# V and K traffic on the GpSimd DMA queue, and one attention step per FFN step, in a fused attention and FFN kernel

## The chip, the cores and the metric

The kernel runs on all 8 cores of one Trainium2 chip. Every core runs the same program on its own quarter of one batch element's rows, and the cores don't exchange anything. The metric is the time of the slowest core in microseconds (us); lower is better.

## The reference

One sandwich layer over x of shape (2, 8192, 1024) in float32: an attention with sigmoid weights, then a five-matrix FFN, each with a layer norm before and after and a residual.

```python
q, k, v = (proj(Wq), proj(Wk), proj(Wv))            # 16 heads of 64
scores = einsum('bhqd,bhkd->bhqk', q, k) * SCALE
w = sigmoid(scores)
w = w / (w.sum(axis=-1, keepdims=True) + EPS)
out = einsum('bhqk,bhkd->bhqd', w, v) ... @ Wo.T
h = silu(x @ w1.T * s1) * (x @ w2.T * s2)            # 1024 -> 4096
h = gelu(h @ h1.T * hs1)                             # 4096 -> 4096
h = gelu(h @ h2.T * hs2)                             # 4096 -> 4096
return h @ w3.T * s3                                 # 4096 -> 1024
# layer: x = x + ln(attention(ln(x)));  x = x + ln(ffn(ln(x)))
```

## The kernel before

Five instruction streams (PE, ACT, DVE, SP, GpSimd) are written out by hand. `emit(eng, fn, waits, incs)` appends one piece to a stream: the engine waits for the semaphore values in `waits`, then runs `fn`. Each stream is executed strictly in the order in which it was emitted. `"sy"` is SP's stream and DMA queue, `"gp"` is GpSimd's (POOL in the profile). A barrier makes SP wait for everything, then all engines for SP.

A core holds S = 8192 rows of x (transposed) and computes the T = 2048 query rows that are its own. The order of the work:

- **Projection stage** (`phase0`), four super-tiles of 2048 rows. Each: the layer norm's statistics (eight loads of `xs`, Square on ACT, sums on PE), the normalised `lnb` (eight more loads of `xs`), K projection (eight blocks, DVE copies to `kvo`, DMA to `K_sc` in HBM, L367), in the first also Q, then V projection: 16 blocks of 128 rows, 16 matmuls each, a DVE cast to `vvo` (L416; two buffers), and a DMA to `V_sc` (L431). This DMA writes rows of 65 bf16 (130 B): 128 partitions x 16 heads = 2048 pieces.
- **Attention A** (`gen_phase1` with `kct` = 3), 2 blocks of 512 queries x 8 head pairs. For each head pair one load of `kbuf` (2 MB, L520), then tiles of key chunks. A tile is: for each of the two heads, score matmuls into `psS` (L561), one sigmoid on ACT into `wtil` (L573), and then the value matmuls of the *previous* tile into `psO` (L600). Every 8 key chunks two loads of `vbuf` (130 KB each, L546; four slots, two per head). At the end of the head pair two row sums go out (`RS_sc`, L625).
- **phase2** for 1024 rows: output projection, layer norm, residual, `y1`. Its last part goes over eight row blocks: load of `xb` (L758), three DVE operations (L762, L765, L768), store of `y1t` to `y1_sc` (L774), statistics.
- **Mixed stage**: attention B (`kct` = 2, one `kbuf`, the other 2 blocks of 512 queries) and FFN A are two generators whose pieces are taken in turn (L219 to L232): two `yield`s of attention, one of the FFN. Attention B has 16 head pairs x 33 = 528 yields (32 tiles of 2 key chunks and a closing one). FFN A has two halves of 512 rows with 232 yields each: w1 32 (8 matmuls, Silu on ACT), w2 32 (8 matmuls, DVE), h1 and h2 64 each (16 matmuls, and a Gelu every second yield), w3 24 (two with 16 matmuls, one without), 8 for statistics, 8 for the output. That makes 464. Its weights come by casting DMAs on GpSimd's queue into two buffers `wfb` (L837): 256 KB each for w1 and w2, 1 MB for h1, h2 and w3; each waits for the matmuls of the weight block two before it.
- **phase2** for the other 1024 rows, then **FFN B** over them in one go.

The semaphores `st_v0` and `st_v1` are used by the V stores of the projection stage and again by the `RS_sc` stores.

Of the kernel before, what the change touches and what calls it, by code (L numbers as in the profile page):

```python
# [20 lines left out]
class Builder:  # L21
# [70 lines left out]
    def build(self):  # L92
# [26 lines left out]
        for s in ["bar", "pe", "act", "dve", "gp",  # L119
                  "ld_x0", "ld_x1",  # L120
                  "ld_w0", "ld_w1", "ld_w2",
                  "ld_k0", "ld_k1",
                  "ld_v0", "ld_v1", "ld_v2", "ld_v3",
                  "ld_y0", "ld_y1",
                  "ld_c",
                  "st_k0", "st_k1",
                  "st_v0", "st_v1",
                  "st_y0", "st_y1",
                  "st_rs",
                  "st_o0", "st_o1"]:  # L130
            self.sem(s)

# [81 lines left out]
        if qms_b:  # L214
            with ExitStack() as pctx:
                psS, psO = p1_psums(pctx, 2, nkb=1)
                g_mid = self.gen_phase1(qms_b, 2, psS, psO)
                g_ffn = gen_ffn_a()
                mid_alive = ffn_alive = True  # L219
                while mid_alive or ffn_alive:  # L220
                    if mid_alive:
                        for _ in range(2):
                            try:
                                next(g_mid)
                            except StopIteration:
                                mid_alive = False
                                break
                    if ffn_alive:
                        try:
                            next(g_ffn)  # L230
                        except StopIteration:
                            ffn_alive = False  # L232
        else:
            for _ in gen_ffn_a():
                pass
# [18 lines left out]
    def phase0(self):  # L254
# [4 lines left out]
        with ExitStack() as sc:  # L259
# [10 lines left out]
            for b in range(2):  # L270
                for hh in range(NH):
                    self.emit("gp", lambda e, b=b, hh=hh: e.memset(
                        vvo[b][:, hh * (DH + 1) + DH: hh * (DH + 1) + DH + 1], 1.0),
                        incs=[("gp", 1)])
# [12 lines left out]
            for sup in range(NSUP):  # L287
                ts0 = sup * TSUP
# [54 lines left out]
                with ExitStack() as pctx:  # L343
                    psP = [pctx.enter_context(nc.psum_tensor(self.u(f"psP{i}"), [128, TSUP], F32))
                           for i in range(2)]
                    psP_free = [[], []]
                    for oc in range(NCD):
                        par = oc % 2

                        def mk_kproj(e, o=oc, p=par, psP=psP):  # L350
                            for ic in range(NCD):
                                for tt in range(NTT):
                                    inst = e.matmul(  # L353
                                        psP[p][:, tt * NT:(tt + 1) * NT],
                                        wkb[:, ic * D + o * 128: ic * D + o * 128 + 128],
                                        lnb[:, ic * TSUP + tt * NT: ic * TSUP + (tt + 1) * NT],
                                        start=(ic == 0), stop=(ic == NCD - 1))
                            return inst
                        self.emit("pe", mk_kproj,
                                  waits=[("dve", ln_ready), ("ld_w0", wproj_ready)] + psP_free[par],  # L360
                                  incs=[("pe", 1)])
                        mmv = self.c("pe")
                        self.emit("dve", lambda e, p=par, psP=psP: e.tensor_copy(kvo[p][:], psP[p][:]),
                                  waits=[("pe", mmv)] + kvo_free[par], incs=[("dve", 1)])
                        psP_free[par] = [("dve", self.c("dve"))]
                        dvv = self.c("dve")
                        self.emit("sy", lambda e, p=par, o=oc, ts0=ts0: e.dma_start(  # L367
                            self.K_sc[o, :, ts0:ts0 + TSUP], kvo[p][:]),
                            waits=[("dve", dvv)], incs=[(f"st_k{par}", 16)])
                        kvo_free[par] = [(f"st_k{par}", self.c(f"st_k{par}"))]  # L370
                    if sup == 0:
                        NTTQ = T // NT
                        for oc in range(NCD):
                            par = oc % 2

                            def mk_qproj(e, o=oc, p=par, psP=psP):
                                for ic in range(NCD):
                                    for tt in range(NTTQ):
                                        inst = e.matmul(
                                            psP[p][:, tt * NT:(tt + 1) * NT],  # L380
                                            wqb[:, ic * D + o * 128: ic * D + o * 128 + 128],
                                            lnb[:, ic * TSUP + tt * NT: ic * TSUP + (tt + 1) * NT],
                                            start=(ic == 0), stop=(ic == NCD - 1))
                                return inst
                            self.emit("pe", mk_qproj,
                                      waits=[("dve", ln_ready), ("ld_w0", wproj_ready)] + psP_free[par],
                                      incs=[("pe", 1)])
                            mmv = self.c("pe")
                            self.emit("dve", lambda e, p=par, o=oc, psP=psP: e.tensor_copy(
                                self.qbuf[:, o * T:(o + 1) * T], psP[p][:, 0:T]),  # L390
                                waits=[("pe", mmv)], incs=[("dve", 1)])
                            psP_free[par] = [("dve", self.c("dve"))]

                with ExitStack() as pctx:
# [3 lines left out]
                    for tk in range(TSUP // 128):  # L398
# [26 lines left out]
                        def mk_vst(e, p=par, tkg=tkg, NKC_ALL=NKC_ALL):  # L425
# [3 lines left out]
                            src = bass.AP(vvo[p], 0,  # L429
                                          [[NH * (DH + 1), 128], [DH + 1, NH], [1, DH + 1]])  # L430
                            return e.dma_start(dst, src)  # L431
                        self.emit("sy", mk_vst, waits=[("dve", dvv)], incs=[(f"st_v{par}", 16)])
                        vvo_free[par] = [(f"st_v{par}", self.c(f"st_v{par}"))]

    def alloc_rows(self, scope, W, tag):
# [57 lines left out]
    def gen_phase1(self, qms, kct, psS, psO):  # L493
# [14 lines left out]
        if True:  # L508
# [7 lines left out]
            for qm in qms:  # L516
                q0 = qm * QM
                for hp in range(NCD):
# [20 lines left out]
                    for ti, (kc0, nk) in enumerate(tiles):  # L539
                        for kc in range(kc0, kc0 + nk):  # L540
                            if kc % 8 == 0:
                                kb = kc // 8
                                for hh in range(2):
                                    vslot = hh * 2 + kb % 2
                                    self.emit("sy", lambda e, hh_=2 * hp + hh, kb=kb, p=vslot:
                                              e.dma_start(vbuf[p][:], bass.AP(  # L546
                                                  self.V_sc.tensor,
                                                  hh_ * 128 * NKC_ALL * (DH + 1) + kb * 8 * (DH + 1),
                                                  [[NKC_ALL * (DH + 1), 128],
                                                   [1, 8 * (DH + 1)]])),  # L550
                                              waits=vbuf_free[vslot],
                                              incs=[(f"ld_v{vslot}", 16)])
                                    v_lds[(hh, kb)] = self.c(f"ld_v{vslot}")
# [65 lines left out]
                    for hh in range(2):  # L619
                        h = 2 * hp + hh  # L620
                        self.emit("dve", lambda e, hh=hh: e.tensor_copy(  # L621
                            rs_row[hh][:], psO[hh][64:65, :]),
                            waits=[("pe", pv_all)] + rs_free[hh], incs=[("dve", 1)])
                        rsd = self.c("dve")
                        self.emit("sy", lambda e, hh=hh, h=h, q=q0: e.dma_start(  # L625
                            self.RS_sc[h:h + 1, q:q + QM], rs_row[hh][:]),
                            waits=[("dve", rsd)], incs=[(f"st_v{hh}", 16)])
                        rs_free[hh] = [(f"st_v{hh}", self.c(f"st_v{hh}"))]
                        self.emit("dve", lambda e, hh=hh, c=hp, q=q0: e.tensor_copy(
                            self.obuf[hh * 64:hh * 64 + 64, c * T + q: c * T + q + QM],  # L630
                            psO[hh][0:64, :]),
                            waits=[("pe", pv_all)], incs=[("dve", 1)])
                        psO_free[hh] = [("dve", self.c("dve"))]
# [3 lines left out]
    def phase2(self, t0, TW, ln2t):  # L637
# [4 lines left out]
        with ExitStack() as sc:  # L642
# [27 lines left out]
            with ExitStack() as pctx:  # L670
# [3 lines left out]
                for c in range(NCD):  # L674
                    par = c % 2
# [73 lines left out]
            with ExitStack() as pctx:  # L749
# [6 lines left out]
                for ic in range(NCD):  # L756
# [14 lines left out]
                        incs=[("dve", 1)])  # L771
                    dvv = self.c("dve")
                    xb_free[par] = [("dve", dvv)]
                    self.emit("sy", lambda e, i=ic, p=par, t0=t0, y1t=y1t: e.dma_start(  # L774
                        self.y1_sc[i, :, t0:t0 + TW], y1t[p][:]),
                        waits=[("dve", dvv)], incs=[(f"st_y{par}", 16)])
                    self.emit("act", lambda e, p=par, sq2=sq2, y1t=y1t: e.activation(
# [367 lines left out]
```

How the kernel before makes its waits and increments, by code:

```python
        def closure(e, fn=fn, wl=wl, il=il):  # L49
            for h, v in wl:
                e.wait_ge(h, v)
            inst = fn(e) if fn is not None else None
            for h, n in il:
                assert inst is not None
                inst.then_inc(h, n)
```

## Time and profile before

| | us |
|---|---|
| median of 2 runs | 8227.16 (8216.3 and 8238.03) |
| the profiled execution | 8052.45 |
| its slowest core (6), from first to last instruction | 8050.9 |
| spans of the eight cores | 7983.0 to 8050.9 |
| projection stage | 0 to 1745 |
| attention A | 1745 to 3050 |
| phase2 | 3050 to 3230 |
| mixed stage | 3230 to 6448 |
| phase2 | 6450 to 6620 |
| FFN B | 6620 to 8050 |

All rows are of core 6. The stage bounds are read from the first and last instructions of each stage's lines. In the profile PE is the matmul row of TensorE and PEld its weight loads; a matmul's own duration is modelled and overlaps its neighbours, so rates are read from the distance between starts. "DMA share" is the mean busy share of the 16 DMA engines.

### The profile page before, as it was taken

To read this page: it belongs to the slowest core of one execution; us is meant where nothing else is said; L and a number is where in the kernel's file an instruction comes from. 1 tells how busy PE (TensorE), PEld (TensorE's weight loads), DVE (VectorE), ACT (ScalarE), POOL (GpSimd) and SP (SyncE) were. 2 spreads that over 40 slices of the span, in tenths; PEclk is the share of its full clock that TensorE was granted. 3 is DMA by queue.
4 is the path that set the end of the run, shared out by engine and by line. 5 is a ranking of instruction groups with operands and counts; after the bars stand their busy time and mean duration, and the time that the engine had idled before them with its cause. 6 is when DMAs were issued, how large, how long until landed. Compare 5 with 4: busy or idle time off the path is not lost.

```text
span 8050.9 us, 66197 instructions; the slowest of 8 cores (7983.0 to 8050.9 us)
## 1 busy us (share of the span) xinstructions
PE 5763.5 (72%) x22567; PEld 2173.6 (27%) x22904; DVE 806.9 (10%) x659; ACT 2656.6 (33%) x2394; POOL 221.1 (3%) x453
## 2 busy tenths in 40 slices
PE   5645354547878786568788788766688757899996
PEld 1212121212222222112222222212233213344442
DVE  2112031300000003001000000010100140100002
ACT  1000000026777772565555555466100011000000
POOL 0000000000000000000000000000100001000000
PEclk7867676778989897779999999987999969999898
DMA  4778777681111112223434333322566524444343
GB/s 125 24 67 58 62 62 64 61 32 57 48 58 48 58 48 61 59 58 71 91 81 83 87 82 83 74 59 48 80 125 127 111 76 62 72 75 77 68 74 76
DMA packets 298831, 570.25 MB, mean 71 GB/s; under 512 B 151328, under 2 KB 216864, under 8 KB 257952
## 3 DMA queue, kind: packets, MB, share of 16 engines
q1 hardware_dynamic: 239056, 278.65, 22.6%
q0 software_dynamic: 59472, 287.34, 20.7%
q8 instruction: 217, 3.56, 0.2%
q14 instruction: 86, 0.70, 0.0%
HBM read 802.49 MB, written 50.72 MB: 106 GB/s over the span
## 4 chain that ended last, share of the span: by engine, by line
PE 53%; DMA 24%; ACT 11%; issue 8%; DVE 4%; SPq 0%; ACTq 0%; DVEq 0%; POOLq 0%
PE psG L902 20%; DMA V_sc<-vvo 10%; PE psS L561 9%; ACT wtil L573 8%; PE psO L600 8%; PE psF L857 5%; DMA kbuf<-K_sc 3%; DMA wfb<-h 3%; PE psP L353 3%; DMA wfb<-w 3%; DMA xs<-xT 3%; PE psW L939 3%; PE ps_sum L306 1%; ACT L573 1%; DMA xb<-xT 1%
## 5 line engine op out<-in xcount | busy, mean ns | idle before, releaser
L573 ACT ACTIVATE wtil<-psS 128x1024 bf16<-128x1024 f32 (+1 forms) x1728 | 1935.7, 1180 | 945.9 <-PE psS L561 941.2
L902 PE MATMUL psG<-fb,wfb 128*128 128x512 bf16 x8005 | 1845.2, 389 | 100.8 <-DMA wfb<-h 80.8
L561 PE MATMUL psS<-qbuf,kbuf 64*128 64x512 bf16 x4096 | 1033.1, 404 | 827.8 <-ACT wtil L573 487.6
L600 PE MATMUL psO<-wtil,vbuf 128*65 128x512 bf16 x4096 | 1140.6, 411 | 12.0 <-ACT wtil L573 12.0
L902 PEld LDWEIGHTS psG<-fb,wfb 128*128 128x128 bf16 x8192 | 814.3, 100 | 1129.3 <-issue 280.7
L561 PEld LDWEIGHTS psS<-qbuf,kbuf 64*128 64x128 bf16 x4096 | 244.2, 95 | 1546.7 <-issue 1470.4
L404 PE MATMUL psV<-wvb,lnb 128*128 128x512 bf16 x1004 | 325.6, 495 | 444.7 <-DVE vvo L416 432.0
L600 PEld LDWEIGHTS psO<-wtil,vbuf 128*65 128x65 bf16 x4096 | 407.2, 116 | 689.0 <-issue 462.7
L300 ACT ACTIVATE sq<-xs 128x2048 bf16<-128x2048 f32 x32 | 61.2, 1911 | 1238.1 <-DMA xs<-xT 1238.1
L621 DVE COPY rs_row<-psO 1x512 f32<-1x512 f32 x64 | 43.8, 684 | 3093.6 <-PE psO L600 3092.5
L353 PE MATMUL psP<-lnb,wkb 128*128 128x512 bf16 x1000 | 227.2, 388 | 158.5 <-DVE lnb L337 157.4
L857 PE MATMUL psF<-ln2tA,wfb 128*128 128x512 bf16 x976 | 292.7, 446 | 61.1 <-DMA wfb<-w 49.4
L915 ACT ACTIVATE fb<-psG,hs2b 128x512 bf16<-128x512 f32 (+1 forms) x96 | 79.7, 830 | 677.8 <-PE psG L902 677.4
L404 PEld LDWEIGHTS psV<-wvb,lnb 128*128 128x128 bf16 x1024 | 120.1, 121 | 650.2 <-issue 598.8
L306 PE MATMUL ps_sum<-xs,onesF 128*1 128x512 f32 x256 | 145.0, 720 | 200.3 <-ACT sq L300 200.3
L857 PE MATMUL psF<-ln2tB,wfb 128*128 128x512 bf16 x1003 | 233.1, 386 | 76.6 <-DMA wfb<-w 66.2
L915 ACT ACTIVATE fb<-psG,hs1b 128x512 bf16<-128x512 f32 (+1 forms) x96 | 79.7, 830 | 629.5 <-PE psG L902 629.1
L939 PE MATMUL psW<-fb,wfb 128*128 128x512 bf16 x1001 | 226.0, 383 | 15.3 <-DMA wfb<-w 9.3
L573 ACT ACT_TABLE_LOAD x128 | 164.2, 1283 | 210.6 <-PE psS L561 209.5
L952 DVE TENSOR_SCALAR fbf<-psW,s3b 128x512 bf16<-128x512 f32 (+1 forms) x24 | 22.3, 929 | 1877.3 <-PE psW L939 1621.8
L857 PEld LDWEIGHTS psF<-ln2tA,wfb 128*128 128x128 bf16 x1024 | 116.1, 116 | 243.2 <-issue 177.0
L353 PEld LDWEIGHTS psP<-lnb,wkb 128*128 128x128 bf16 x1024 | 101.9, 100 | 288.1 <-issue 172.8
(103 smaller groups left out, 2116.0 us busy)
## 6 DMA issues: line engine op xcount, KB each, us to landing
wfb<-h POOLq DMA_DIRECT2D x192, 1024.0 KB, 8.2
vbuf<-V_sc SPq DMA_DIRECT2D x512, 130.0 KB, 2.7
xs<-xT SPq DMA_DIRECT2D x64, 1024.0 KB, 4.8
kbuf<-K_sc SPq DMA_DIRECT2D x32, 2048.0 KB, 8.2
wfb<-w POOLq DMA_DIRECT2D x192, 256.0 KB, 3.8
wfb<-w POOLq DMA_DIRECT2D x24, 1024.0 KB, 8.3
V_sc<-vvo SPq DMA_DIRECT2D x64, 260.0 KB
K_sc<-kvo SPq DMA_DIRECT2D x32, 512.0 KB, 2.6
```

The source lines that it names most:

```text
L300: lambda e, p=par: e.activation(sq[p][:], xs[p][:], AF.Square),
L306: e.matmul(ps_sum[0:1, tt * NT:(tt + 1) * NT], self.onesF[:], xs[p][:, tt * NT:(tt + 1) * NT], start=(i == 0), stop=(i == NCD - 1))
L353: inst = e.matmul(psP[p][:, tt * NT:(tt + 1) * NT], wkb[:, ic * D + o * 128: ic * D + o * 128 + 128], lnb[:, ic * TSUP + tt * NT: ic * TSU ...
L404: inst = e.matmul(psV[p][:, oh * NT:(oh + 1) * NT], lnb[:, ic * TSUP + t * 128: ic * TSUP + t * 128 + 128], wvb[:, ic * D + oh * NT: ic * ...
L561: inst = e.matmul(psS[hh][:, j * QM:(j + 1) * QM], kbuf[kp][b:b + 64, (k0 + j) * 128:(k0 + j + 1) * 128], self.qbuf[b:b + 64, hp_ * T + q0 ...
L573: self.emit("act", lambda e, w=w, hh=hh, n=nk: e.activation(wtil[w][:, 0:n * QM], psS[hh][:, 0:n * QM], AF.Sigmoid, scale=ATT_SCALE), wait ...
L600: inst = e.matmul(psO[hh][:, :], vbuf[vslot][:, a_ * (DH + 1): a_ * (DH + 1) + DH + 1], wtil[w][:, j * QM:(j + 1) * QM], start=(k == 0), s ...
L621: self.emit("dve", lambda e, hh=hh: e.tensor_copy(rs_row[hh][:], psO[hh][64:65, :]), waits=[("pe", pv_all)] + rs_free[hh], incs=[("dve", 1)])
L857: inst = e.matmul(psF[p][:, tt * NT:(tt + 1) * NT], wfb[b][:, ic * 128:(ic + 1) * 128], ln2t[:, ic * ln2_w + off + tt * NT: ic * ln2_w + o ...
L902: inst = e.matmul(psF[p][:, tt * NT:(tt + 1) * NT], wfb[b][:, ic * 128:(ic + 1) * 128], s[:, ic * th + tt * NT: ic * th + (tt + 1) * NT], ...
L915: self.emit("act", lambda e, o=oc, p=par, d=dstb, sc_=scl, psF=psF: e.activation(d[:, o * th:(o + 1) * th], psF[p][:], AF.Gelu, scale=sc_[ ...
L939: inst = e.matmul(psF[p][:, tt * NT:(tt + 1) * NT], wfb[b][:, ic * 128:(ic + 1) * 128], fb1[:, ic * th + tt * NT: ic * th + (tt + 1) * NT] ...
```

## The change

Five edits. The K and V stores of the projection stage (L367, L431), the 512 loads of `vbuf` (L546) and the 16 stores of `y1t` (L774) are issued by GpSimd instead of SP. The stores of the row sums get semaphores of their own, `st_r0` and `st_r1`. In the mixed stage one attention yield is taken per FFN yield, not two.

```diff
-                  "st_rs",
+                  "st_rs", "st_r0", "st_r1",
...
                     if mid_alive:
-                        for _ in range(2):
-                            try:
-                                next(g_mid)
-                            except StopIteration:
-                                mid_alive = False
-                                break
+                        try:
+                            next(g_mid)
+                        except StopIteration:
+                            mid_alive = False
...
-                        self.emit("sy", lambda e, p=par, o=oc, ts0=ts0: e.dma_start(
+                        self.emit("gp", lambda e, p=par, o=oc, ts0=ts0: e.dma_start(
                             self.K_sc[o, :, ts0:ts0 + TSUP], kvo[p][:]),
...
-                        self.emit("sy", mk_vst, waits=[("dve", dvv)], incs=[(f"st_v{par}", 16)])
+                        self.emit("gp", mk_vst, waits=[("dve", dvv)], incs=[(f"st_v{par}", 16)])
...
-                                    self.emit("sy", lambda e, hh_=2 * hp + hh, kb=kb, p=vslot:
+                                    self.emit("gp", lambda e, hh_=2 * hp + hh, kb=kb, p=vslot:
                                               e.dma_start(vbuf[p][:], bass.AP(
...
-                            waits=[("dve", rsd)], incs=[(f"st_v{hh}", 16)])
-                        rs_free[hh] = [(f"st_v{hh}", self.c(f"st_v{hh}"))]
+                            waits=[("dve", rsd)], incs=[(f"st_r{hh}", 16)])
+                        rs_free[hh] = [(f"st_r{hh}", self.c(f"st_r{hh}"))]
...
-                    self.emit("sy", lambda e, i=ic, p=par, t0=t0, y1t=y1t: e.dma_start(
+                    self.emit("gp", lambda e, i=ic, p=par, t0=t0, y1t=y1t: e.dma_start(
                         self.y1_sc[i, :, t0:t0 + TW], y1t[p][:]),
```

## Rows read from the trace of the kernel before

**Rows 1.** Windows by stage: length, busy of each engine, PE clock, DMA share, GB/s.
```profile
core 6: us, PE busy (x) PEld busy (x) DVE busy (x) ACT busy (x) POOL busy (x), PEclk, DMA share, GB/s
282.00:500.00 218.00, 85.54 (x251) 30.95 (x256) 20.02 (x17) 0.00 (x0) 0.00 (x0) 0.67 1.13 19
...
3261.00:5681.00 2420.00, 1805.31 (x7063) 626.70 (x7178) 92.84 (x133) 1409.54 (x1413) 89.50 (x169) 0.88 0.33 71
5683.00:6448.00 765.00, 581.93 (x2522) 247.71 (x2574) 49.26 (x69) 52.63 (x77) 54.07 (x102) 0.95 0.64 115
...
3823.00:5019.00 1196.00, 944.97 (x3924) 344.89 (x3989) 22.63 (x33) 677.77 (x679) 33.47 (x64) 0.92 0.40 84
...
7387.00:7506.00 119.00, 118.42 (x542) 53.93 (x552) 0.00 (x0) 8.91 (x8) 4.24 (x8) 1.00 0.40 72
```

**Rows 2.** Timeline of DVE in the first V projection: third and last cast of 16.
```profile
305.98 1.23 DVE L416 CAST vvo<-psV 128x1024 bf16<-128x1024 f32 x1 [13.18 <-DMA V_sc<-vvo]
...
493.37 1.23 DVE L416 CAST vvo<-psV 128x1024 bf16<-128x1024 f32 x1 [11.91 <-DMA V_sc<-vvo]
```

**Rows 3.** Timeline of POOL, mixed stage: one weight load each of w1, w2, h1, w3.
```profile
3354.28 0.53 POOL L837 DMA_DIRECT2D wfb<-w  x1 [9.87 <-PE psS L561]
3691.43 0.53 POOL L837 DMA_DIRECT2D wfb<-w  x1 [5.54 <-PE psS L561]
3923.28 0.53 POOL L837 DMA_DIRECT2D wfb<-h  x1 [16.34 <-PE psO L600]
5152.67 0.53 POOL L837 DMA_DIRECT2D wfb<-w  x1 [19.40 <-PE psS L561]
```

**Rows 4.** Timeline of PE (first row) and ACT, mixed stage, h1, around one Gelu.
```profile
3929.33 0.59 PE L561 MATMUL psS<-qbuf,kbuf 64*128 64x512 bf16 x2 [1.61 <-ACT wtil L573]
...
3924.25 0.69 ACT L915 ACTIVATE fb<-psG,hs1b 128x512 bf16<-128x512 f32 x1
3926.86 1.28 ACT L573 ACT_TABLE_LOAD   x1 [1.93 <-PE psS L561]
3928.16 3.85 ACT L573 ACTIVATE wtil<-psS 128x1024 bf16<-128x1024 f32 x4
```

**Rows 5.** Timeline of PE where a head pair ends.
```profile
5211.33 1.24 PE L561 MATMUL psS<-qbuf,kbuf 64*128 64x512 bf16 x4 [10.69 <-DMA kbuf<-K_sc]
```

**Rows 6.** Timeline of POOL after attention B ended: first and last of 62 h1/h2 loads.
```profile
5805.58 0.53 POOL L837 DMA_DIRECT2D wfb<-h  x1 [15.27 <-PE psG L902]
...
6311.27 0.53 POOL L837 DMA_DIRECT2D wfb<-h  x1 [7.13 <-PE psG L902]
```

**Rows 7.** Timeline of ACT, w3: two tiles back to back without FFN work between.
```profile
5132.89 1.94 ACT L573 ACTIVATE wtil<-psS 128x1024 bf16<-128x1024 f32 x2 [0.20 <-PE psS L561]
5135.09 1.94 ACT L573 ACTIVATE wtil<-psS 128x1024 bf16<-128x1024 f32 x2 [0.27 <-PE psS L561]
```

**Rows 8.** Page: DMA issues, with KB each and median us from issue to landing.
```profile
wfb<-h POOLq DMA_DIRECT2D x192, 1024.0 KB, 8.2
vbuf<-V_sc SPq DMA_DIRECT2D x512, 130.0 KB, 2.7
...
wfb<-w POOLq DMA_DIRECT2D x192, 256.0 KB, 3.8
```

**Rows 9.** Page: packets by size, software queue; tile wfb: POOL's DMA instruction, min/median/max ns.
```profile
DMA packets 298831, 570.25 MB, mean 71 GB/s; under 512 B 151328, under 2 KB 216864, under 8 KB 257952
...
q0 software_dynamic: 59472, 287.34, 20.7%
...
L837 POOL DMA_DIRECT2D wfb<-h x192: 530/530/539, 3817.5 to 7825.3; - x192
```

**Rows 10.** Timeline of PE where the second super-tile's statistics begin.
```profile
512.23 5.48 PE L306 MATMUL ps_sum<-xs,onesF 128*1 128x512 f32 x8 [39.64 <-ACT sq L300]
```

**Rows 11.** Waits, whole span: who waited, for whom, us in total, times, longest us.
```profile
DVE y1t L768 <- DMA xb<-xT: 43.1, 14, 4.7
```

## The prediction

> **What bounds the kernel now.** I read the times of the cores first (all within 0.9%, so one core may stand for all), then the windows by stage, then the timeline inside each stage that the change touches. The reader is to see three things.
>
> First, in the V projection PE is busy 85.5 of 218 us while the DMA engines are full at 19 GB/s [rows 1]. The third to the sixteenth cast into `vvo` come (493.37 - 305.98) / 13 = 14.4 us apart and each waits for a V store [rows 2]. So a V store costs 14.4 us of the DMA engines, in four super-tiles.
>
> Second, the mixed stage has two parts: 2420 us in which two attention tiles go with each FFN step, and 765 us in which the FFN is alone because attention B has run out [rows 1]. A matmul at full clock is 119 / 542 = 0.2196 us [rows 1]. A tile has 8 matmuls (1.75 us), an h step 16 (3.5 us), a w1 or w2 step 8 (1.75 us). The distance between weight loads gives the cadence; add 0.53 to the idle time in brackets: w1 10.40 us, w2 6.07, h 16.87 per block of two steps, w3 19.93 per block [rows 3]. PE work alone would be 5.25, 5.25, 14.0 and 17.5. The rest is the ping-pong: with two tiles in a row the second tile's scores wait for the first one's sigmoid, 1.61 us where a table load lies before it [rows 4]. Around each Silu and Gelu ACT loads a table twice, 1.28 us each. Where a head pair ends, PE stands 10.7 us for the single `kbuf` [rows 5].
>
> Third, in the part where the FFN is alone, h blocks come (6311.27 - 5805.58) / 61 = 8.3 us apart [rows 6], against 7.0 us of matmuls: weights bound it, and ACT idles.
>
> **The change, part by part.** The largest is the ratio of 1:1. FFN A has 464 steps, attention B 528. After the change 464 pairs of one tile and one FFN step run, then 64 attention steps alone. Only one tile stands between FFN steps, so its sigmoids are hidden behind the FFN's matmuls. Step by step:
>
> - w1, 64 steps. ACT needs per step a table load, a Silu, a table load and two sigmoids: 1.29 + 0.70 + 1.29 + 1.95 = 5.2 us, from the durations of [rows 4] with the Gelu's for the Silu. PE needs 3.5. ACT bounds; I take 5.3. 64 x 5.3 = 339, and two to three head pair ends of about 8 each (ACT catches up part of the 10.7): 362.
> - w2, 64 steps: PE 3.5, ACT 1.95, DVE less. 64 x 3.5 = 224, two ends at 10.7: 245.
> - h, 128 blocks of two steps: PE 2 x (1.75 + 3.5) = 10.5; ACT 4 x 0.97 + 1.29 + 0.70 + 1.29 = 7.2. After a Gelu the next sigmoid is done 0.1 + 1.29 + 0.70 + 1.29 + 0.97 = 4.35 us after the matmuls, and its `psS` is wanted after 5.25, so PE doesn't wait. 128 x 10.5 = 1344. Before, the window of h had 1196 us for 63 cadences of 16.87 = 1063 us: 12.5% on top for `kbuf` and low-clock stretches (clock 0.92) [rows 1]. The same share gives 168: 1512.
> - w3, 16 blocks of three tiles and 32 matmuls: 12.25 + 0.5 for the one pair of tiles left in a row; with two ends 227.
> - Statistics, 16 steps of tile and Square at 3.7: 64. Two row computations at 15: 30. Output, 16 steps at the pace of sigmoids, 2.2 us a tile [rows 7]: 40.
> - New: at the output of half 0 the DVE chain (about 4 us per row block, 32 us) is no longer covered by 16 tiles but by 8, and the first w1 load of half 1 waits for it: 17.
> - The 64 steps alone: 62 tiles x 2.2 = 136 and two ends: 156. Drain: 8.
>
> The sum is 362 + 245 + 1512 + 227 + 64 + 30 + 40 + 17 + 156 + 8 = 2661 us, against 3187 from the same start (2420 + 2 + 765). Gain: 526. That ACT gets some 128 more table loads (half 1's Gelus now stand between sigmoids), 164 us, is in the sum: in h ACT has 3 us to spare per block.
>
> The `vbuf` loads go behind weight loads on one queue. GpSimd then waits in order. A V load waits for value matmuls four steps back; a weight load waits for the block two before, which ended two steps back (w) or three (h). So the V load is issued at least two steps before its turn and wanted one step after it: over 10 us in w, over 15 in h. It lands in 2.7 us, behind a 1 MB load in about 8.2 + 0.8 more [rows 8]. A weight load in h has 3 tiles + one block of matmuls = 12.2 us before it is wanted, and lands in 8.2; in w 5.25 against 3.8 [rows 8]. Cost 0; if the cover in w1 and w2 were gone, 128 steps would each pay up to 1 us. In attention A no V load is waited for by PE now, and three tiles of slack remain: 0. SP's `kbuf` loads stay behind the `RS_sc` stores as they were, so the 10.7 us at each head pair stay too. The new semaphores cost nothing: they only part two uses that lie in different stages.
>
> The V stores are the unknown. Their 64 x 2048 = 131072 pieces make up most of the 151328 packets under 512 B [rows 9]. The queue that GpSimd issues to has 413 DMAs and 59472 packets now, 144 each, and POOL spends 530 ns on one [rows 9]; no row shows it with 2048 pieces. If all of the 530 ns went with the 128 rows, 2048 pieces would take 16 x 0.53 = 8.5 us of POOL; if none did, 0.53. Both are below 14.4, and with two buffers one store can be prepared while the other drains, so I take 0. The ends: preparing and draining one after the other, 8.5 us on each of the 56 waiting casts, +476; or stores that drain as fast as they can be prepared, (14.4 - 8.5) x 56 = 330 less. K stores (32 of 128 rows) take POOL 0.53 us each, and a block of 32 matmuls (7 us) lies over each: 0.
>
> DVE is busy for 20 of the 218 us of a V projection [rows 1]. The Trainium skill (SBUF — State Buffer, section SBUF: two separate sides) speaks against the move: DMAs issued from GpSimd starve while DVE runs an operation that takes the port pair the two share, and the page advises SP's or ACT's queue. By that rule the worst is those 20 us in each of four super-tiles, 80 in all; whether this cast from PSUM takes that port no row here shows. The sum goes without it.
>
> With the V stores off SP, the first two `xs` loads of a super-tile no longer stand behind the last store. PE's sums now begin at 512.23 [rows 10]; they must wait for the last cast, done at 493.37 + 1.23 = 494.6 [rows 2]. That is 17.6 us, less some competition with the stores still draining: 13 x 3 super-tiles = 40.
>
> In phase2 an `xb` load stood behind the `y1t` store of the block before, and DVE waited 43.1 us for it in all [rows 11]. With the store on GpSimd that wait goes, and about 8 come back since the store's landing now gates `y1t`: 35.
>
> Sum: 526 + 40 + 35 = 601. 8052 - 601 = 7451 us in the profiled execution's own terms. The median of the runs is 8227.16 / 8052.45 = 1.0217 of it, so the number to compare is 7451 x 1.0217 = 7613, say 7610.
>
> **Rivals.** *GpSimd bounds the V projection* (the one that can end slower). Place: the 56 casts that wait for a store. For it: 2048 pieces in a pattern of three dimensions is not what the 530 ns row shows. Against: even at the full 8.5 us the DMA engines' 14.4 last longer. Serial with the drain, at 22.9 us a store, it costs 476: 7927, times 1.0217 8099, 1.6% under now. The point from which the kernel is slower by 2% is 8391 / 1.0217 = 8213, so (8213 - 7451) / 56 = 13.6 us more, 28 us a store, or 1.75 us of POOL per 128 pieces, 3.3 times the row. At 35 us a store it would be 7451 + 1150 = 8601, times 1.0217 8790.
>
> *Queueing spoils the 1:1 stage*: weight loads come late behind V loads and `kbuf`. For it: w has only 1.4 us of slack. Against: DMA share 0.40 in h [rows 1]. If w paid 1 us and h blocks 1.5 us each: 128 + 192 = 320 less gain, 7771 x 1.0217 = 7940.
>
> *The clock eats it*: PE is busier, and the clock in the mixed stage was 0.88, alone 0.95 [rows 1]. Against: w2 and h cadences are constant at full clock apart from head pair ends. At 0.88 over the whole 2100 us of matmuls: up to 150 less, 7601, times 1.0217 7766. *V stores run faster on the other queue*, at 8.5 us: 330 more, 7121, times 1.0217 7276. Nothing in the rows speaks for it but the ends of the bound.
>
> **How the numbers follow.** As summed, with small misses either way 0.66; GpSimd as the bound 0.14 (0.07 up to 24 us a store, 0.07 beyond); queueing 0.08; clock 0.08; faster stores 0.04. Two per cent is about what a measurement of this kernel can tell. Faster by over 2%: the first and the last three, 0.86, and a little of the GpSimd case (under 22 us), 0.02; within 2%: 0.05; slower: 0.07. Range: 7330 (the runs at the profile's 7451 and some of the faster stores) to 7830 (the clock's loss, a third of the way to the serial stores). Below it lie most of the faster stores, above it half of the queueing case and most of the GpSimd case.
>
> **What would show it.** Windows: mixed stage 2660 us long with no FFN-only part of 765. POOL's weight loads 5.3 (w1), 3.5 (w2) and 10.5 us (h) apart. V casts still 14.4 us apart and POOL at most 8.5 us at a V store. First sums of a super-tile within 5 us of the last cast. `y1t` not waiting for `xb`. Wrong, if POOL is solid with V stores, if PE waits for `wfb` or `vbuf` in the mixed stage, or if h blocks take over 12 us.

## The result, and the profile after

The changed kernel takes 7522.61 us (median of 12 runs, 7297.37 to 7749.68), the kernel before 8241.57 us (median of 10 beside them): ratio 0.8957, 95% interval 0.8856 to 0.9058. That is faster by 10.4%; forecast were 7610 us and 7.5%.

In some executions, the changed kernel's profiled one among them (its cores 4 to 7), cores of one die or both run at a lower clock; the two medians count these executions, while ratios, and the times of the experiments below, leave them out. Readings from here on, of either kernel, are of core 2 where nothing else is said. The quotient of the two medians is 0.913, that of core 2's spans 0.911, and runs repeated below give 0.907 to 0.909, just above the interval; so the change is worth nearer 9% than 10.4%, and why the first ratio came out lower stayed open. Cores of the changed kernel, spans and granted clock:

```profile
core 2: 7278.4 us, clock 0.872
...
core 7: 7418.9 us, clock 0.854
die 0 (median of its cores): 7278.4 us, clock 0.872
die 1 (median of its cores): 7376.8 us, clock 0.854
```

On core 2 the kernel before spans 7992.0 us, the changed one 7278.4: 714 us less. The windows tell where they were. The stages in order are projection, attention A, phase2, mixed stage, phase2, FFN B; columns as in [rows 1]. Before:

```profile
0.00:1717.00 1717.00, 844.49 (x2776) 304.23 (x2776) 360.92 (x188) 77.75 (x42) 3.77 (x43) 0.73 0.76 63
1717.00:3017.00 1300.00, 1021.85 (x4112) 354.70 (x4112) 43.80 (x64) 945.16 (x706) 0.00 (x0) 0.90 0.17 53
3017.00:3232.00 215.00, 125.43 (x308) 40.81 (x308) 86.69 (x68) 27.75 (x27) 0.54 (x1) 0.67 0.27 81
3232.00:6424.00 3192.00, 2404.16 (x9756) 877.65 (x9756) 142.41 (x202) 1463.04 (x1491) 144.18 (x272) 0.90 0.41 81
6424.00:6622.00 198.00, 118.57 (x280) 38.06 (x280) 86.83 (x68) 20.72 (x20) 0.53 (x1) 0.67 0.25 75
6622.00:7992.00 1370.00, 1247.31 (x5672) 553.58 (x5672) 86.05 (x69) 121.28 (x109) 72.09 (x136) 0.97 0.40 74
```

After:

```profile
0.00:1680.00 1680.00, 833.48 (x2776) 300.78 (x2776) 361.22 (x188) 77.69 (x41) 95.09 (x139) 0.73 0.49 64
1680.00:2975.00 1295.00, 1020.55 (x4114) 354.75 (x4115) 43.79 (x64) 945.30 (x706) 138.14 (x257) 0.90 0.16 53
2975.00:3180.00 205.00, 118.78 (x300) 39.77 (x298) 87.19 (x68) 25.82 (x25) 5.91 (x12) 0.68 0.29 84
3180.00:5733.00 2553.00, 2199.80 (x9765) 835.79 (x9766) 142.51 (x202) 1627.51 (x1620) 283.83 (x527) 0.92 0.50 102
5733.00:5919.00 186.00, 111.28 (x280) 37.41 (x278) 87.45 (x68) 21.97 (x21) 4.69 (x9) 0.70 0.29 80
5919.00:7278.00 1359.00, 1244.00 (x5672) 552.28 (x5672) 86.04 (x69) 121.05 (x109) 72.23 (x136) 0.97 0.41 75
```

The reader is to see: of the 714 us, 639 are the mixed stage's, 37 the projection stage's, 22 the two phase2's. The remaining 16 lie in attention A and FFN B, where next to nothing was changed. PE has the same matmuls but 204 us less busy time in the mixed stage (91 of them in the scores, 47 in the value matmuls), ACT 164 us more (the table loads of half 1), POOL 140 us more.

Inside the mixed stage, POOL's weight loads of the changed kernel, w1, w2 and h1 (the rows answering to [rows 3]; the distance from one start to the next is the load's 0.53 plus the idle time, and 1.10 more where V loads stand between):

```profile
3244.11 0.54 POOL L835 DMA_DIRECT2D wfb<-w  x1 [4.71 <-PE psF L855]
3249.36 0.53 POOL L835 DMA_DIRECT2D wfb<-w  x1 [4.71 <-PE psF L855]
...
3405.89 0.54 POOL L835 DMA_DIRECT2D wfb<-w  x1 [2.70 <-PE psS L559]
3409.18 0.53 POOL L835 DMA_DIRECT2D wfb<-w  x1 [2.75 <-PE psS L559]
...
3577.76 0.54 POOL L835 DMA_DIRECT2D wfb<-h  x1 [9.42 <-PE psO L598]
3578.29 1.10 POOL L544 DMA_DIRECT2D vbuf<-V_sc  x2
3587.75 0.54 POOL L835 DMA_DIRECT2D wfb<-h  x1 [8.36 <-PE psO L598]
```

So w1 steps come 5.25 us apart, w2 steps 3.29 in these rows and mostly 3.25, h blocks 9.99 in these rows (median 9.95). Against forecasts of 5.3, 3.5 and 10.5 the first holds and the others are too long. From the first and last loads of each part:

| | before | forecast | after |
|---|---|---|---|
| w1, 64 steps | 660 | 362 | 330 |
| w2, 64 steps | 340 | 245 | 244 |
| h1 and h2, 128 blocks | 1743 | 1512 | 1385 |
| w3, statistics, output, attention tail | 449 | 542 | 594 |
| mixed stage | 3192 | 2661 | 2553 |

PE's timeline of one h block shows why 10.5 was too long:

```profile
3612.54 3.62 PE L900 MATMUL psG<-fb,wfb 128*128 128x512 bf16 x16
3616.09 0.61 PE L559 MATMUL psS<-qbuf,kbuf 64*128 64x512 bf16 x4
3616.63 1.05 PE L598 MATMUL psO<-wtil,vbuf 128*65 128x512 bf16 x4
3617.52 3.62 PE L900 MATMUL psG<-fb,wfb 128*128 128x512 bf16 x16
```

Four score matmuls take 3616.63 - 3616.09 = 0.54 us, not 4 x 0.22 = 0.88. A tile costs 1.43 us, not 1.75.

The V stores. POOL's instruction in the view of the tile `V_sc` (min/median/max ns), and the page's packet row (answering to [rows 9]), both of core 7:

```profile
L429 POOL DMA_DIRECT2D V_sc<-vvo x64: 1152/1152/1177, 289.5 to 1679.2; - x64
```

```profile
DMA packets 122704, 570.25 MB, mean 77 GB/s; under 512 B 20256, under 2 KB 20256, under 8 KB 81824
```

Timeline of DVE, third and last cast of the first super-tile (to [rows 2]):

```profile
295.08 1.23 DVE L414 CAST vvo<-psV 128x1024 bf16<-128x1024 f32 x1 [4.99 <-DMA V_sc<-vvo]
...
481.92 1.23 DVE L414 CAST vvo<-psV 128x1024 bf16<-128x1024 f32 x1 [12.66 <-DMA V_sc<-vvo]
```

POOL spends 1.15 us on a store of 2048 pieces, between the bounds of 0.53 and 8.5 and near the lower. The casts are (481.92 - 295.08) / 13 = 14.4 us apart, as before. The 131072 small packets are gone from the count and yet the stores take as long.

### The profile page after: what moved, and what is told of

The parts are those of the page before. It is cut to its first block, busy times and chain, and to the rows that moved or that the text cites. A ratio compares the mean times of both kernels' runs of the same rounds, so it can differ in the third digit from the quotient of the medians.

```text
span 7418.9 us, 66672 instructions; the slowest of 8 cores (7269.4 to 7418.9 us)
## 1 busy us (share of the span) xinstructions
PE 5669.7 (76%) x22904; PEld 2152.9 (29%) x22904; DVE 807.7 (11%) x659; ACT 2819.7 (38%) x2522; POOL 597.8 (8%) x1077
## 2 busy tenths in 40 slices
DMA packets 122704, 570.25 MB, mean 77 GB/s; under 512 B 20256, under 2 KB 20256, under 8 KB 81824
## 4 chain that ended last, share of the span: by engine, by line
PE 60%; DMA 21%; ACT 8%; issue 6%; DVE 5%; SPq 0%; ACTq 0%; DVEq 0%; POOLq 0%
PE psG L900 25%; DMA V_sc<-vvo 10%; PE psO L598 10%; PE psS L559 9%; ACT wtil L571 6%; PE psF L855 4%; DMA kbuf<-K_sc 4%; PE psW L937 4%; PE psP L351 3%; DMA xs<-xT 2%; DMA wfb<-w 2%; PE ps_sum L304 1%; DMA y1f<-y_sc 1%; PE psA L702 1%; PE psB L677 1%
## 5 line engine op out<-in xcount | busy, mean ns | idle before, releaser
L900 PE MATMUL psG<-fb,wfb 128*128 128x512 bf16 x8192 | 1877.2, 389 | 22.0 <-DMA wfb<-h 12.0
L559 PE MATMUL psS<-qbuf,kbuf 64*128 64x512 bf16 x4096 | 946.9, 405 | 525.8 <-DMA kbuf<-K_sc 353.3
L598 PE MATMUL psO<-wtil,vbuf 128*65 128x512 bf16 x4096 | 1107.5, 402 | 3.6 <-ACT wtil L571 3.2
L559 PEld LDWEIGHTS psS<-qbuf,kbuf 64*128 64x128 bf16 x4096 | 227.3, 95 | 1186.6 <-issue 1110.1
L544 POOL DMA_DIRECT2D vbuf<-V_sc x512 | 276.8, 544 | 1585.1 <-PE psO L598 1501.3
L855 PE MATMUL psF<-ln2tA,wfb 128*128 128x512 bf16 x1024 | 275.1, 417 | 20.6 <-DMA wfb<-w 19.9
L937 PE MATMUL psW<-fb,wfb 128*128 128x512 bf16 x1024 | 269.0, 430 | 8.8 <-ACT fb L913 8.8
L835 POOL DMA_DIRECT2D wfb<-h x192 | 102.5, 534 | 2112.6 <-PE psO L598 1168.8
```

The lines of the kernel that those rows point to most:

```text
L544: e.dma_start(vbuf[p][:], bass.AP(self.V_sc.tensor, hh_ * 128 * NKC_ALL * (DH + 1) + kb * 8 * (DH + 1), [[NKC_ALL * (DH + 1), 128], [1, 8 ...
L559: inst = e.matmul(psS[hh][:, j * QM:(j + 1) * QM], kbuf[kp][b:b + 64, (k0 + j) * 128:(k0 + j + 1) * 128], self.qbuf[b:b + 64, hp_ * T + q0 ...
L598: inst = e.matmul(psO[hh][:, :], vbuf[vslot][:, a_ * (DH + 1): a_ * (DH + 1) + DH + 1], wtil[w][:, j * QM:(j + 1) * QM], start=(k == 0), s ...
L835: self.emit("gp", lambda e, s=src_ap, b=b, w=width: e.dma_start(wfb[b][:, 0:w], s), waits=wfb_free[b], incs=[(f"ld_w{b}", 16)])
L855: inst = e.matmul(psF[p][:, tt * NT:(tt + 1) * NT], wfb[b][:, ic * 128:(ic + 1) * 128], ln2t[:, ic * ln2_w + off + tt * NT: ic * ln2_w + o ...
L900: inst = e.matmul(psF[p][:, tt * NT:(tt + 1) * NT], wfb[b][:, ic * 128:(ic + 1) * 128], s[:, ic * th + tt * NT: ic * th + (tt + 1) * NT], ...
```

## The experiments

Each kernel ran beside runs of the kernel before on the same chip. The three groups ran on three chips, and the kernel before differs among them by 2%, so times are compared within one. Group 1 (before: 7885 to 7898 us): the ratio alone, the queues alone, scores apart, grouped V stores.

### The ratio alone

```diff
 (the kernel before)
-                        for _ in range(2):
-                            try:
-                                next(g_mid)
...
+                        try:
+                            next(g_mid)
```

> The kernel before with the 1:1 ratio alone; K, V and y1 traffic stays on SP's queue. Theory: nearly all of the gain is the ratio's. On core 2 the changed kernel gained 714 us, 649 of them between the start of the first phase2 and the end of the mixed stage, some 17 of these in phase2. So the mixed stage is about 630 us shorter than before, h blocks come 9.96 us apart and w2 blocks 3.25, the projection stage is unchanged at 1717 us (core 2), and the kernel takes 0.915 to 0.93 of the time before. Rival: the V loads on GpSimd's queue let the 1:1 stage run; then h blocks take 11 us or more here and the gain is under 500 us.

Measured: ratio 0.9169 (0.9147 to 0.9191). The cadences of w1, w2 and h are 5.25, 3.25 and 9.95 us, those of the changed kernel, and the mixed stage is 5652 - 3101 = 2551 us long. The theory holds: the gain of the mixed stage needs nothing from the queues. The projection stage ended at 1592 us, not at the 1717 expected: on this chip the V casts are 12.0 to 12.5 us apart with the stores still on SP's queue, so V stores are quicker here by themselves.

### The queues alone

```diff
 (the changed kernel)
-                        try:
-                            next(g_mid)
...
+                        for _ in range(2):
+                            try:
+                                next(g_mid)
```

> The changed kernel with the old 2:1 ratio. Theory: the queue moves are worth 40 us in the projection stage, some 35 in the two phase2 and next to nothing elsewhere: 80 us or 1% in all, ratio 0.985 to 0.995; cadences in the mixed stage as before (10.40, 6.07, 16.87 us). Rival: they are worth 200 us or more because a V or K store on GpSimd's queue lets the stages overlap better; or V loads behind weight loads cost something at 2:1 and the ratio is above 1.

Measured: 0.9895 (0.9872 to 0.9919), inside the theory's range. Cadences 10.40, 6.07 and 16.87 us as before. The product of the two, 0.9169 x 0.9895 = 0.907, lies just above the interval of the whole change (0.8856 to 0.9058).

### Scores apart

```diff
                             psS_free[hh] = [("act", sig_done[hh])]
+                            if hh == 0 and pending_pv is not None:
+                                pending_pv()
-                        if pending_pv is not None:
-                            pending_pv()
```

> The changed kernel, but the value matmuls of the previous tile are emitted between the score matmuls of the first and of the second head. Same work, same engines. Theory: the score matmuls of two heads (rows 0 to 63 and 64 to 127 of the array) run side by side when they follow each other, 4 in 0.54 us against 4 x 0.22 = 0.88; apart they can't. Then an h block takes 9.96 + 2 x 0.34 = 10.6 us and a w2 block 3.6, and the mixed stage is 128 x 0.68 + 64 x 0.34 + 16 x 1.0 = about 125 us longer; attention A gets longer too, since the second head's sigmoid starts 0.9 us later. Rival: score matmuls are simply short (64 rows) and cost 0.13 us each wherever they stand; h blocks stay at 9.96 us.

Measured: 0.9604 (0.9549 to 0.9660) of the time before, so 5 to 6.5% slower than the changed kernel's 0.907. h blocks are 11.22 us apart, w2 steps 3.89. PE's timeline of this kernel:

```profile
3606.07 0.60 PE L559 MATMUL psS<-qbuf,kbuf 64*128 64x512 bf16 x2
3606.60 1.05 PE L597 MATMUL psO<-wtil,vbuf 128*65 128x512 bf16 x4
3607.59 0.60 PE L559 MATMUL psS<-qbuf,kbuf 64*128 64x512 bf16 x2
3608.12 3.63 PE L899 MATMUL psG<-fb,wfb 128*128 128x512 bf16 x15
```

Two score matmuls take 0.53 us here, four took 0.54 in the changed kernel: the two heads' scores do run side by side, and the rival falls. The size was under-estimated, 0.63 us a tile, not 0.34: a lone pair takes 0.53, not 0.44, and the value matmuls 0.99, not 0.89. An estimate from these rows is that each change between 64-row and 128-row matmuls costs some 0.1 us (0.53 less 2 x 0.22, 0.99 less 4 x 0.22). The mixed stage takes 2830 us, not 2551, so 279 more where 125 were expected: 140 more in h, 32 in w2, and 107 in its last part, where tiles stand in a row. Attention A takes 1427 us, not 1293. In those two the second head's sigmoid also starts later, and its share was not parted from that of the lost overlap.

### Grouped V stores

```diff
-            vvo = [... [128, NH * (DH + 1)] ...]
+            VG = 4
+            VW = VG * (DH + 1)
+            vvo = [... [128, NH * VW] ...]
...
-                            dst = bass.AP(vvo[p], 0, [[NH * (DH + 1), 128], [DH + 1, NH], [1, DH]])
+                            dst = bass.AP(vvo[vp], vg * (DH + 1), [[NH * VW, 128], [VW, NH], [1, DH]])
...
+                        if vg != VG - 1:
+                            continue
```

> The changed kernel, with the V stores of four row blocks put into one: vvo holds four blocks, and a store writes 2048 pieces of 520 B, not 130 B; 16 stores, not 64. Same bytes, same queue. Theory: a V store is bound by its pieces, 14.4 us per 2048 whatever their size, so it takes 3.6 us per row block and the V projection is bound by PE at about 3.6 us per block: 60 to 80 us per super-tile, not 210, some 560 us less in all, ratio to before about 0.83. Rival: it is bound by bytes at 19 GB/s (260 KB in 14.4 us); then a grouped store takes 57 us and the projection stage stays within 30 us of 1680.

(The ones beside V's columns are also set by one memset per buffer here, no longer by sixteen.)

Measured: 6681.9 us in a single execution, against 7885.4 of the kernel before, 0.847; there are too few runs for an interval. The two last casts of a super-tile in DVE's timeline, and the store's row among the DMA issues, with its median landing:

```profile
336.57 1.22 DVE L415 CAST vvo<-psV 128x1024 bf16<-128x1024 f32 x1 [2.23 <-PE psV L401]
340.02 1.23 DVE L415 CAST vvo<-psV 128x1024 bf16<-128x1024 f32 x1 [2.23 <-PE psV L401]
```

```profile
V_sc<-vvo POOLq DMA_DIRECT2D x16, 1040.0 KB, 9.1
```

Casts are 3.45 us apart and wait for PE, not for a store; the projection stage ends at 1068 us, against 1551 with scores apart beside it, whose stage is the changed kernel's. That is 483 less, and not the 560 expected, since V casts on this chip were only some 12 us apart. The rival (bytes) falls: 1040 KB land in 9.1 us, where 260 KB took some 12.

What one piece costs stayed open. The same grouped store, of 2048 pieces of 520 B, takes a median of 11.8 us to land on another chip (group 3), and 14.3 us from SP's queue on a third (group 2), where stores of 2048 pieces of 130 B come 14.1 us apart. In that last kernel its landings spread from 6.3 to 19.2 us:

```profile
DMA to landing us min/median/max: 6.3/14.3/19.2
```

So a piece has no fixed price, and that a piece of 520 B is cheaper than one of 130 B is not shown; that a store of as many pieces takes about as long with four times the bytes is. The Trainium skill (DMA: Bandwidth & Descriptors, Specifications) gives 512 B as the least size for line rate, below which the engine reads, modifies and writes. The gain from 130 B to 520 B goes the way of that rule; no run here shows the reading and modifying, and none has a size between the two.

Group 2 (before: 8024 and 8029 us): the changed kernel again and three variants of it.

### The changed kernel again, V stores on SP, V loads on SP, grouped stores on SP

> The changed kernel once more, as the yardstick for the kernels beside it. Expected: 0.9169 x 0.9895 = 0.907 of the time before, the product of its two parts run alone. If the parts need each other, it is under 0.90; if they get in each other's way, over 0.915.

Measured: 7296.6 and 7302.3 us, 7299 / 8026 = 0.909: the two parts neither need each other (under 0.90) nor get in each other's way (over 0.915).

```diff
-                        self.emit("gp", mk_vst, ...
+                        self.emit("sy", mk_vst, ...
```

> The changed kernel with the 64 V stores back on SP's queue. Theory: a V store costs the same on either queue (the casts stay as far apart as in the changed kernel beside it, within the spread of 1 us that runs of one kernel show), and what the move gave is that the xs loads of the next super-tile come early: last cast to first cast of the next super-tile was 195 to 202 us with the move and 204 to 213 us without. So +9 to +12 us at each of three super-tiles, 30 to 35 us, 0.4%. Rival: the stores themselves run slower on SP's queue, by 0.5 us or more each: then 28 us or more on top, and the casts are 0.5 us further apart.

Measured: 7344.9 to 7348.1 us, 43 to 51 more, where 30 to 35 were expected. Mean distance of the casts in the four super-tiles 14.0 to 14.3 us, against 13.2 to 14.2 in the changed kernel beside it, and 13.9 to 15.0 in its first profile: no difference that is clear of the spread, though 0.3 us on average over 56 casts would be some 20 us, and the rival's share stays open. Last cast to next first cast: 213 to 215 us, against 194 to 204. The first sums of the second super-tile, in the changed kernel and in this one; the last casts before them were at 477.35 and 476.34:

```profile
478.87 4.89 PE L304 MATMUL ps_sum<-xs,onesF 128*1 128x512 f32 x8 [19.65 <-DVE vvo L414]
```

```profile
507.42 6.37 PE L304 MATMUL ps_sum<-xs,onesF 128*1 128x512 f32 x8 [53.74 <-ACT sq L298]
```

In the changed kernel they start 0.3 us after the last cast has ended, here 29.9 us after it. Only some 15 us of that reach the next first cast, since the sums after the first ones wait for their own `xs` loads. What the move is worth is the order of SP's queue, some 15 us at each of three super-tiles.

```diff
-                                    self.emit("gp", lambda e, hh_=2 * hp + hh, kb=kb, p=vslot:
+                                    self.emit("sy", lambda e, hh_=2 * hp + hh, kb=kb, p=vslot:
```

> The changed kernel with the 512 vbuf loads back on SP's queue. Theory: no wait in the mixed stage ends with a V load on either queue, so nothing changes: within 10 us, cadences 9.96 and 3.25 us as before. Rival: the waits of GpSimd's queue for V loads delay weight loads (POOL waited 1501 us in front of vbuf loads); then PE's wait for wfb shrinks from 12 us and the mixed stage gets shorter by 20 us or more here.

Measured: 7300.4 and 7311.4 us against 7296.6 and 7302.3. Nothing, and PE's wait for h weights is 20.1 us, against 17.1 in the changed kernel beside it. The move of the `vbuf` loads did neither good nor harm.

> Four row blocks per V store as in the grouped kernel, but these 16 x 4 stores issued by SP. Theory: pieces bound a store, not the queue; casts stay 3.45 us apart (PE's own pace), the kernel takes as long as the grouped one on GpSimd's queue plus up to 35 us for late xs loads. Rival: 520 B pieces run at line rate only from GpSimd's queue, which puts several into one packet; then the casts are 5 us or more apart on SP's.

Measured: 6757.0 us, in one execution. Casts 3.45 us apart on SP's queue too, and 209 to 211 us from the last cast to the next first one, against 187 to 188 with the stores on GpSimd's. The store's row in this kernel:

```profile
V_sc<-vvo SPq DMA_DIRECT2D x16, 1040.0 KB, 14.3
```

The rival falls as far as the casts go: grouping makes the gain on either queue. But 14.3 us to land, against 9.1 from GpSimd's queue in group 1, leaves room for it in the store itself. Nothing waits for that here, because a grouped store has four casts, 13.8 us, of time and a second buffer; chip and queue differ together, so neither is shown to be the reason.

Group 3 (before: 7882 and 7889 us).

### y1 stores on SP

```diff
-                    self.emit("gp", lambda e, i=ic, p=par, t0=t0, y1t=y1t: e.dma_start(
+                    self.emit("sy", lambda e, i=ic, p=par, t0=t0, y1t=y1t: e.dma_start(
```

> The changed kernel with the 16 y1t stores back on SP's queue. Theory: DVE waits for xb again, 39 to 43 us in all over both phase2, and the wait for the store's landing (12.5 us in the changed kernel) goes; from wob's load to the first w1 load of the mixed stage it takes 215 us as before the change, not 205, and the second phase2 198, not 186: some 21 us together. Rival: the y1 move is worth the full 35 us of the sum and something else in phase2 took 14 back; then more than 30 us.

Measured: from `wob`'s load to the first w1 load 213 us, second phase2 196: 8 and 10 us more than in the changed kernel's first profile, near the 21 expected and far from the rival's 30. The K stores were the only ones not moved back by themselves. Waits of DVE in this kernel, then in the changed one:

```profile
DVE y1t L766 <- DMA xb<-xT: 37.5, 14, 3.1
```

```profile
DVE y1t L760 <- DMA y_sc<-y1t: 12.5, 9, 2.3
```

### K loaded ahead

```diff
 (the grouped kernel; load_k is new)
+                        if whole:                       # two kbufs, attention A
+                            if ti == 1:
+                                load_k(seq + 1, 0)
+                        elif (kc0 + nk) % 16 == 0:      # one kbuf, in quarters
+                            load_k(seq + 1, (kc0 + nk) // 16 - 1)
```

> The grouped kernel (four row blocks per V store) with K loaded ahead: in attention A the next head pair's kbuf load is issued after the second tile, not behind the last row sums; in attention B the single kbuf is loaded in four quarters, each as soon as the scores have used it up. Same bytes. Theory: PE's waits for kbuf (349 us over 30 head pairs in the changed kernel) go almost entirely, and the time falls by 300 to 350 us against the grouped kernel beside the same yardstick, to about 0.81 of the time before. Rival: part of that wait is covered anyway, or the loads then collide with weight loads (1 MB every 10 us): the gain is under 200 us and PE waits for wfb by over 60 us in the mixed stage.

Measured: 6366.0 and 6366.9 us, 0.807 of the 7886 beside it, and 316 less than the grouped kernel's 6682 (of group 1, whose runs of the kernel before agree with these). PE's waits for `kbuf` in the changed kernel:

```profile
PE psS L559 <- DMA kbuf<-K_sc: 348.9, 30, 27.4
```

In this kernel none of these 30 is left, only the waits for the two loads at the head of each attention part (51.5 us; 88.6 in the changed kernel, beside the 348.9). Attention A takes 1110 us, not 1290, the mixed stage 2400, not 2564, and PE waits 30.4 us for h weights, not 60 or more. This is the fastest kernel of the study.

### K loaded ahead, and every seventh step two tiles

```diff
-                        try:
-                            next(g_mid)
...
+                    for _ in range(2 if stp % 7 == 0 else 1):
```

> As the kernel with K loaded ahead, and every seventh FFN step takes two attention steps, so that both generators end together (464 x 8 / 7 = 530 against 528) and no attention tail is left. Theory: 64 tiles at 2.2 us alone become tiles inside the mix; one placed second in a row costs 0.99 us more than its 1.42 (its scores wait for the sigmoid and run apart), about 2.4 us: hardly any gain, within 30 us of the kernel beside it. Rival: the tail's 2.2 us against 1.42 us is all saved: 50 us less.

Measured: 6453 us, in one execution, against 6366 of the kernel above: 87 us slower. The theory allowed 30 either way, and the rival has the wrong sign. The timelines of PE and then ACT where the second tile follows a Gelu:

```profile
2838.72 3.62 PE L937 MATMUL psG<-fb,wfb 128*128 128x512 bf16 x16
2842.27 0.61 PE L590 MATMUL psS<-qbuf,kbuf 64*128 64x512 bf16 x4
2842.81 1.05 PE L635 MATMUL psO<-wtil,vbuf 128*65 128x512 bf16 x4
2845.47 0.59 PE L590 MATMUL psS<-qbuf,kbuf 64*128 64x512 bf16 x2 [1.61 <-ACT wtil L602]
...
2847.79 3.62 PE L937 MATMUL psG<-fb,wfb 128*128 128x512 bf16 x16
```

```profile
2843.01 1.28 ACT L602 ACT_TABLE_LOAD   x1 [1.02 <-PE psS L590]
```

From one `psG` to the next it is 9.07 us, not 4.98: the second tile costs 4.09 us after a Gelu. Alone in the tail it costs 2.2. The table load sits between the first tile's scores and its sigmoid, and the second tile's scores wait for both, and then run apart. Over the stage (2503 us, not 2400) h takes 151 us more for its 37 or so second tiles, 4.1 each on average, and w1 and w2 together 64 more; what came after them gives 112 back, less than both.

## Why the prediction was right, and where its sizes were off

**The ratio.** Right in mechanism, and shown so by the ratio alone, which gives 0.917 by itself. The step "a tile has 8 matmuls (1.75 us)" was mis-sized. A tile whose two heads' scores follow each other costs 1.43 us. In the kernel before only the first tile of each pair did so; the second's scores waited for two sigmoids in turn. So 1:1 gained twice, by hiding the sigmoids and by letting every tile's scores run side by side. Against the forecast, which counted only the first of these, the second is 128 x 0.54 = 69 us in h and 64 x 0.25 = 16 in w2 (where the head pair ends took it back); scores apart shows the effect by itself. The surcharge for `kbuf` and clock in h was 1385 - 128 x 9.95 = 111 us, not 168: some 7.75 head pairs end in h before and after, and the surcharge was scaled by time where it goes by head pairs.

**w1** was bound by ACT at 5.25 us, as worked out from its rows; the total was 330, not 362, so the head pair ends cost nothing there.

**The end of half 0.** The step gave 17 us for an uncovered DVE chain in front of the first w1 load. The cost came about a little differently:

```profile
4377.24 1.24 PE L559 MATMUL psS<-qbuf,kbuf 64*128 64x512 bf16 x4 [27.36 <-DMA kbuf<-K_sc]
```

A head pair ended just there. The `RS_sc` stores and the next `kbuf` load stood on SP behind the output stores, which wait for that chain: PE stood 27.4 us, some 17 more than at an ordinary end.

The last row of the table is 594, not 542. Its parts were not measured one by one; half 0 has 224 us where the forecast's terms come to 198, half 1 370 where they come to 345, and which of them were too short stayed open.

**V stores.** Taken at 0, and V casts are as far apart as before (14.4). POOL's part was bounded by 0.53 and 8.5 us, and is 1.15. The rival that could end slower needed 28 us a store; nothing of it was seen. By the rule of the Trainium skill (SBUF — State Buffer, SBUF: two separate sides) that DMAs issued from GpSimd starve under a DVE operation on the shared port pair, the move would have cost up to 80 us. The cadence shows no such loss (12.0 to 12.5 us on SP's queue and 10.5 to 12.2 on GpSimd's, both in group 1), and the profile doesn't tell whether this cast takes that port. The prediction read the 14.4 us as what a store costs the DMA engines; the grouped kernel shows that it goes by how a store is cut into pieces, and its landings, which spread, that it isn't a fixed cost.

**xs and y1t.** 40 us were forecast for the `xs` loads; the projection stage gained 37, and with the stores back on SP it lost some 15 a super-tile. The first sums begin 0.3 us after the last cast, as forecast; the gain is less than the 18 to 28 us of core 2 that this saves, because later `xs` loads bind. For phase2, 35 were forecast and 22 came: the wait for `xb` went, but 12.5 us of wait for the store's landing took part of its place.

**The V loads** cost 0 and brought 0, as said. PE did wait for weights in the mixed stage, which the prediction gave as a sign of being wrong, but for 31 us in all, against 140 before the change.

**The median.** The sum was carried to the runs with a factor of 1.0217. Against core 2's gain of 714 the sum was 113 us short. With 714 in its place the same factor gives (8052 - 714) x 1.0217 = 7497, and the median is 7523, so nearly all of the 87 us by which 7610 was too long is the sum's. That the factor held is luck in part, since it was taken from two runs and one profile of the kernel before. The five executions of the changed kernel that count for the ratio take 7297 to 7383 us, three of them less than the range's lower end of 7330.

## What to carry to other kernels

When two streams of work are woven together, look at what stands next to what, not only at the sum: one tile between two blocks of matmuls hides its activation, a second tile in a row waits for it and for the table load before it. A ratio that ends both streams together is not better if it puts two in a row. And where a DMA stage runs far below its bandwidth, look at the size of its pieces before its queue: here the queue of the V stores was worth 0.6%, and pieces of 520 B instead of 130 B 7 to 8%.

## What the runs showed of the hardware

- Score matmuls on 64 rows, two for each of two row halves, take 0.54 us for four and 0.53 for two; a change between them and 128-row matmuls costs some 0.1 us (an estimate from scores apart).
- POOL spends 1.15 us to issue a store of 2048 pieces, of 130 B or of 520 B, and 0.53 us for one of 128 rows.
- Issued by GpSimd, 2048 pieces of 130 B are no longer seen as packets under 512 B (151328 before, 20256 after), and drain no faster.
- V stores of 130 B pieces are 10.5 to 12.5 us apart in groups 1 and 3 and 13.2 to 15.0 in the first profiles and group 2, on either queue. What makes them differ stayed open. Grouped stores of 520 B pieces land in 9.1, 11.8 and 14.3 us in the three groups (medians of core 2).
- A table load on ACT takes 1.28 us. Where it falls between a tile's scores and its sigmoid, a second tile in a row costs PE 4.09 us, not the 2.2 of the tail.
